# Cross-attention with eight-wide heads on one core: the score matmuls for the softmax maxima as 32-row strips instead of block diagonals

## The reference

```python
Q = _split_heads(q @ Wq.T)          # q = layernorm(x)
K = _split_heads(k @ Wk.T)          # k = v = ctx
V = _split_heads(v @ Wv.T)
scores = einsum('bhqd,bhkd->bhqk', Q, K) / HEAD_DIM ** 0.5
scores = where(attention_mask == 0, NEG_INF, scores)
attn = softmax(scores, axis=-1)
out = einsum('bhqk,bhkd->bhqd', attn, V)     # heads side by side again
x = x + out @ Wo.T
x = x + ffn_top2_of_8(layernorm(x))  # silu(h @ w1.T) * (h @ w3.T) @ w2.T
```

## Time and profile before

| what | value |
|---|---|
| median of 3 runs | 288.39 us (286.16 to 289.48) |
| span of the profiled execution, first to last instruction | 289.2 us |
| quartet 0: front, ticks | to 23.2 us, 23.2 to 40.0 |
| quartet 1: front, ticks | 40.0 to 47.0, 47.0 to 71.0 |
| quartet 2: front, ticks | 71.0 to 78.0, 78.0 to 103.0 |
| quartet 3: front, ticks | 103.0 to 109.0, 109.0 to 147.0 |
| last ticks (`u` = 4) | 147.0 to 182.8 |
| experts and results | 182.8 to 289.2 |

### The profile page before, as it was taken

One profiled execution on the slowest core, in us unless ns is written; L12 is line 12 of the kernel. 1 busy time (PEld: TensorE's weight loads), 2 busy tenths in 40 slices (PEclk: granted clock), 3 DMA queues, 4 the chain that ended last, 5 costly groups with the idle time before them and its releaser, 6 DMA issues.

```text
span 289.2 us, 5289 instructions
## 1 busy us (share of the span) xinstructions
PE 220.1 (76%) x1445; PEld 161.4 (56%) x1445; DVE 214.5 (74%) x619; ACT 131.9 (46%) x291; POOL 109.8 (38%) x120
## 2 busy tenths in 40 slices
PE   0787779998989988887667674688787789997620
PEld 0663456666757665665336542477566668886410
DVE  4779966688759867895977786568895568775596
ACT  5777127554665448342145546243334435453300
POOL 4310350121403070105486556104556565555530
PEclk9996579999999999979756799589899999999855
DMA  6954411353033302331602110421342232211807
GB/s 216 318 233 118 131 35 28 92 125 86 9 98 96 94 0 67 87 100 47 207 9 67 46 39 29 99 47 30 77 79 76 82 84 73 80 52 26 236 5 217
DMA packets 38108, 26.33 MB, mean 91 GB/s; under 512 B 4748, under 2 KB 35726, under 8 KB 37696
## 3 DMA queue, kind: packets, MB, share of 16 engines
q1 hardware_dynamic: 34848, 19.76, 25.5%
q0 software_dynamic: 2656, 5.40, 6.1%
q10 hardware_dynamic: 576, 0.83, 0.9%
HBM read 12.32 MB, written 6.31 MB: 64 GB/s over the span
## 4 chain that ended last, share of the span: by engine, by line
PE 42%; DVE 30%; issue 10%; SPq 8%; DMA 4%; ACT 2%; POOL 1%; another core or an unknown queue 1%; DVEq 0%; ACTq 0%; POOLq 0%
SPq L427 8%; PE bank L528 8%; DVE m_neg L1411 6%; PE bank L759 4%; PE bank L760 3%; PE bank L733 3%; PE bank L652 3%; DMA bd<-st 3%; PE bank L746 3%; PE bank L736 3%; PE bank L693 2%; PE bank L676 2%; PE bank L734 2%; PE bank L679 2%; PE bank L534 2%
## 5 line engine op out<-in xcount | busy, mean ns | idle before, releaser
L1411 DVE TENSOR_REDUCE m_neg<-bank 128x4 f32<-128x512 f32 x64 | 43.5, 684 | 15.4 <-PE bank L693 15.0
L1048 POOL DMA_INDIRECT ys<-big x39 | 38.1, 976 | 40.0 <-DVE big L1447 19.2
L923 ACT ACTIVATE big<-bank 128x512 f32<-128x512 f32 x64 | 37.4, 597 | 20.9 <-PE bank L679 20.0
L797 ACT ACTIVATE st<-bank 128x128 fp32r<-128x128 f32 (+1 forms) x78 | 22.6, 330 | 31.6 <-PE bank L746 16.1
L1004 POOL DMA_INDIRECT xg<-rows,rows_i x24 | 24.6, 1027 | 31.8 <-DVE rows_i L1218 11.6
L693 PE MATMUL bank<-bd,st 128*128 128x512 f32 x64 | 31.1, 509 | 4.7 <-DMA bd<-st 3.8
L676 PE MATMUL bank<-m_bd,ones_b 128*128 128x512 f32 x64 | 31.3, 489 | 2.1 <-ACT big L923 1.9
L759 PE MATMUL bank<-bd,st 128*128 x78 | 24.3, 332 | 9.8 <-DVE big L1447 6.2
L1355 DVE SCALAR_TENSOR_TENSOR st<-st_hi,cst,bank 128x512 fp32r<-128x512 f32 x32 | 23.3, 747 | 11.3 <-ACT st_hi L797 9.0
L1026 POOL TENSOR_TENSOR m_bd<-mT,cst 128x512 fp32r<-128x512 f32 x16 | 17.3, 1110 | 30.1 <-DVE mT L1334 30.0
L679 PE MATMUL bank<-bd,st 128*128 128x512 f32 x64 | 27.1, 423 | 0.0
(11 more groups left out here) (174 smaller groups left out, 514.0 us busy)
## 6 DMA issues: line engine op xcount, KB each, us to landing
bd<-st SPq DMA_DIRECT2D x126, 64.0 KB, 2.0
big<-xg SPq DMA_DIRECT2D x39, 64.5 KB
raw<-in_L_ffn_w SPq DMA_DIRECT2D x2, 1024.0 KB, 9.3
raw<-ys SPq DMA_DIRECT2D x6, 256.0 KB
x_all<-in_x SPq DMA_DIRECT2D x4, 256.0 KB, 4.5
rows<-in_mask_BxS_if POOLq DMA_DIRECT2D x4, 256.0 KB, 5.2
ctx_all<-in_L_ffn_w SPq DMA_DIRECT2D x1, 1024.0 KB
ctx_all<-in_ctx SPq DMA_DIRECT2D x3, 256.0 KB, 5.2
```

The lines of the kernel that those rows point to most:

```text
L923: nc.scalar.activation(prob[n % 2][:, NJ * g:NJ * (g + 1), :].rearrange("p h q -> p (h q)"), s2[k % 2][:, :], ACT.Exp, scale=SCALE).then_i ...
L1048: pool.indirect_dma_start(ys, bass.IndirectOffsetOnAxis(xt[n % XR][:, D:RW].bitcast(I32), 0), y_sb[n % YR], None, bounds_check=PAIRS - 1, ...
L1411: nc.vector.tensor_reduce(m_neg[:, H * (b - 1) + NJ * g:H * (b - 1) + NJ * (g + 1)], s1[k % s1_ring(u)][:, :].rearrange("p (j q) -> p j q" ...
```

## The change

The `s1` product no longer uses a block diagonal. At tick `g` the strip of 32 rows that holds head j = g of all four stacks is used by itself: four matmuls of 32 rows, 128 columns of weights (queries) and 128 moving columns (keys), one for each group i, each into its quarter of the same bank. All four lie on the same strip of the array (`tile_position=(32 g, 0)`); tick by tick the strip moves on. So what a bank holds at tick g is heads (i, g) for i = 0 to 3 instead of heads (g, j), and the reduce writes its four results 4 apart. The block diagonals of the keys go: 62 DMAs of SP, 2 of POOL and their waits, three clears of ACT, and the interleaved order of the remaining DMAs. Two waits for `s1` are dropped, and one for `s2` is added ahead of the fifth piece of expert weights, since `w3_lo` lies in the stacks.

```diff
-        def bd_slot(k, n):
+        def bd_slot(n):
 
-            return bd[:, 3 * (1 - k) + n % 3, :].rearrange("p (g j q) -> p g j q", g=NG, j=NJ)
+            return bd[:, 3 + n % 3, :].rearrange("p (g j q) -> p g j q", g=NG, j=NJ)
...
-            def block_diagonal(k, n):
+            def block_diagonal(n):
 
                 u, b = divmod(n, QB)
-                stacks_in(sp, u, k)
+                stacks_in(sp, u, 0)
                 if n >= 3:
 
-                    sp.wait_ge(s1_full if k else s2_full, NG * (n - 2))
+                    sp.wait_ge(s2_full, NG * (n - 2))
                 else:
-                    sp.wait_ge(bd_cleared, 3 if k else 6)
-                for j in range(2 if k and n == 0 else NJ):
+                    sp.wait_ge(bd_cleared, 3)
+                for j in range(NJ):
...
-                for k, b in ((1, 0), (1, 1), (1, 2), (0, 3), (1, 3)):
-                    if k and u < NQ:
-                        block_diagonal(1, QB * u + b)
-                    if not k and u >= 1:
-                        block_diagonal(0, QB * (u - 1) + b)
+                if u >= 1:
+                    block_diagonal(QB * (u - 1) + 3)
                 if u < NQ:
-                    block_diagonal(0, QB * u)
-                    block_diagonal(0, QB * u + 1)
-                    block_diagonal(0, QB * u + 2)
+                    for b in range(3):
+                        block_diagonal(QB * u + b)
...
-                            if g == 0:
-                                if b == 1:
-                                    stacks_in(pe, u, 0)
-                                    stacks_in(pe, u, 1)
-                                diagonal_in(pe, 1, n)
+                            rows = slice(R * g, R * (g + 1))
+                            if b == 1 and g == 0:
+                                stacks_in(pe, u, 0)
+                                stacks_in(pe, u, 1)
                             if k >= s1_ring(u):
                                 pe.wait_ge(max_done, k - s1_ring(u) + 1)
-                            nc.tensor.matmul(s1[k % s1_ring(u)][:, :], st[:, u % 2, 0, g, (b - 1) * S:b * S],
-                                             bd_slot(1, n)[:, g, :, :].rearrange("p j q -> p (j q)"),
-                                             start=True, stop=True).then_inc(s1_full, 1)
+                            for i in range(NG):
+                                last = nc.tensor.matmul(s1[k % s1_ring(u)][:, i * P:(i + 1) * P], st[rows, u % 2, 0, i, (b - 1) * S:b * S],
+                                                        st[rows, u % 2, 1, i, (b - 1) * S:b * S], start=True, stop=True, tile_position=(R * g, 0))
+                            last.then_inc(s1_full, 1)
...
-            clear_diagonal(0)
-            clear_diagonal(1)
+            act.wait_ge(in_c, 16)
...
-                    act.wait_ge(s1_full, NG * B)
...
-            clear_diagonal(2)
...
-            stacks_in(pool, 0, 1)
-            pool.wait_ge(bd_cleared, 3)
-            for j in range(2, NJ):
-                rows = slice(R * j, R * (j + 1))
-                pool.dma_start(bd_slot(1, 0)[rows, :, j, :].bitcast(F32), st[rows, 0, 1, :, 0:S].bitcast(F32)).then_inc(first_half, 16)
...
+                if k == NB // 4:
+                    dve.wait_ge(s2_full, NG * QB * (NQ - 1))
...
-                            nc.vector.tensor_reduce(m_neg[:, H * (b - 1) + NJ * g:H * (b - 1) + NJ * (g + 1)],
-                                                    s1[k % s1_ring(u)][:, :].rearrange("p (j q) -> p j q", j=NJ), X, ALU.max,
+                            nc.vector.tensor_reduce(m_neg[:, H * (b - 1):H * b].rearrange("p (i j) -> p i j", j=NJ)[:, :, g],
+                                                    s1[k % s1_ring(u)][:, :].rearrange("p (i q) -> p i q", i=NG), X, ALU.max,
                                                     negate=True).then_inc(max_done, 1)
```

More of the change, by code:

```diff
@@ L345, in program @@
         bd_cleared = sem("bd_cleared")
-        kbd_ready = [sem(f"kbd_ready{k}") for k in range(3)]
         qbd_ready = [sem(f"qbd_ready{k}") for k in range(3)]
@@ L349, in program @@
         mhl_ready = sem("mhl_ready")
-        first_half = sem("first_half")
         mbd_ready = sem("mbd_ready")
@@ L377, in stacks_in, with diagonal_in @@
                     taken(engine, ("st", u, k))
[L379 to L383, removed]
+        def diagonal_in(engine, n):
+            engine.wait_ge(qbd_ready[n % 3], 16 * NJ * (n // 3 + 1))
         x_d = x.rearrange("(u b) s d -> u s b d", b=QB)
@@ L414, in _ @@
                 sp.dma_start(raw[k], w).then_inc(in_w13, 16)
-            def block_diagonal(k, n):
+            def block_diagonal(n):
                 u, b = divmod(n, QB)
-                stacks_in(sp, u, k)
+                stacks_in(sp, u, 0)
                 if n >= 3:
-                    sp.wait_ge(s1_full if k else s2_full, NG * (n - 2))
+                    sp.wait_ge(s2_full, NG * (n - 2))
                 else:
-                    sp.wait_ge(bd_cleared, 3 if k else 6)
-                for j in range(2 if k and n == 0 else NJ):
+                    sp.wait_ge(bd_cleared, 3)
+                for j in range(NJ):
                     rows = slice(R * j, R * (j + 1))
-                    sp.dma_start(bd_slot(k, n)[rows, :, j, :].bitcast(F32), st[rows, u % 2, k, :, b * S:(b + 1) * S].bitcast(F32)
-                                 ).then_inc((kbd_ready if k else qbd_ready)[n % 3], 16)
+                    sp.dma_start(bd_slot(n)[rows, :, j, :].bitcast(F32), st[rows, u % 2, 0, :, b * S:(b + 1) * S].bitcast(F32)
+                                 ).then_inc(qbd_ready[n % 3], 16)
             for u in range(NQ + 1):
@@ L668, in _ @@
                             if g == 0:
-                                diagonal_in(pe, 0, n)
+                                diagonal_in(pe, n)
                             if k >= 2:
@@ L679, in _ @@
                             nc.tensor.matmul(s2[k % 2][:, :], st[:, (u - 1) % 2, 1, g, b * S:(b + 1) * S],
-                                             bd_slot(0, n)[:, g, :, :].rearrange("p j q -> p (j q)"),
+                                             bd_slot(n)[:, g, :, :].rearrange("p j q -> p (j q)"),
                                              start=False, stop=True).then_inc(s2_full, 1)
@@ L1346, in _ @@
                         for n in range(QB * (u - 1) - 3, QB * (u - 1)):
-                            diagonal_in(dve, 1, n)
-                            diagonal_in(dve, 0, n)
+                            diagonal_in(dve, n)
                     for k, (is_k, g) in enumerate(stacks(u)):
```

## The result

| | before | changed |
|---|---|---|
| median | 288.94 us (6 runs, 286.16 to 291.12) | 302.48 us (6 runs, 301.54 to 318.81) |
| ratio, 95% interval | | 1.051 (1.044 to 1.057) |
| a repetition: ratio, 95% interval | | 1.046 (1.035 to 1.058) |

The change costs 13.5 us; 300.4 was forecast, with 291 to 313 as the range. The profile shown is of the same kernel run again: span 300.3 us, clock 0.859. Where both are listed, a time lies 1.8 us above the span (302.14 and 300.3), so the profiled execution of before, span 289.2, took about 291 us. It was 2 us above its median, not 0.8 as the prediction has it.

A forecast was written before the change was run, and what follows sets the result against it. PE was taken to bound quartets 1 and 2; stage terms of -0.2, +4.6, +5.2 and +2.4 us summed to +12.0 on 289.2, so 301.2 us profiled and 300.4 for the median, range 291 to 313.

The forecast's parts named there:

- What bounds: PE bounds the ticks of quartets 1 and 2, DVE quartet 0; in quartet 3 they take turns.
- Removal, 1.95 us: Waits for block diagonals that come off: 0.2 us in quartet 0, 1.75 us in quartets 1 to 3.
- The added tick, +0.45 and +0.25: PE time four strips add per tick through weight loads and form changes: +0.45 us, or +0.25 at g = 1.
- the way back: Return from strips to full matmuls in each tick: 0.25 us from the last strip's start.
- Rival 1: Strips change form for free and overlap: +0.20 us a tick, 293.4 us in all; chance 0.19.
- rival 2: No load overlap within a strip: 0.16 us a pair, about +0.60 a tick, 313 us in all; chance 0.14.
- Rival 3: A 32-row weight load costs a quarter, strips stream at 0.055 us: faster, 284.8 us in all; chance 0.07.
- rival 4: Slower 128-column streaming, or half clock in quartets 1 and 2: +0.9 us a tick, 322 us; chance 0.08.
- By stage: Net change of the ticks per quartet: -0.2, +4.6, +5.2 and +2.4 us for quartets 0 to 3, +12.0 in sum.
- Quartet 0's missing gain: PE starts its first `s1` 0.8 us earlier, mostly beside DVE's memset; 0.2 us taken as gain.
- mean of 0.40: Average added PE time over the four ticks g of a batch: +0.40 us a tick.
- The base: The profiled execution, 289.2 us, was taken as 0.8 us above the median of the runs.

The follow-up runs named there:

- x3: The changed kernel with each tick's four strips replaced by one full 128-row matmul of 512 columns on the undivided stacks, no key diagonals: 286.82 us, 0.997 of before.
- x4: The changed kernel with each tick's four strips replaced by four full 128-row matmuls of 128 columns, a weight load each: 290.47 us, 1.005 of before.
- x7: The changed kernel with each tick's four strip matmuls replaced by one of 32 rows and 512 columns: 298.46 us, 1.035 of before.
- x1: The changed kernel run again without edit, for a profile at full clock: 302.51 us, 1.046 of before.
- x10: The kernel before with strips in quartet 0 alone and key diagonals from quartet 1 on: 290.74 us, 1.011 of before.
- x6: The changed kernel with the strips of two ticks issued together at every odd g, alternating between two strips and banks: 306.45 us, 1.064 of before.
- x8: As x6, but the four matmuls of the first strip are issued before the four of the second: 306.59 us, 1.062 of before.

## Why the prediction was right

By its own steps:

- **What bounds**: right. Quartets 1 and 2, where PE was 90% busy and more, took 10.4 of the 13.6 us.
- **Removal, 1.95 us**: right in total (x3: 2.1 us between medians, interval from a gain of 0.7% to a loss of 0.2%). By place it was less good: x3 is 0.5 us shorter than before in quartet 1 (I had 1.0), 0.5 in quartet 2 (0.35) and not shorter in quartet 0 (0.2). In quartet 1 the second wait stood ahead of the ticks of b = 4. Against the first profile, x3 takes 1.0 us less up to their first `s1` (13.4 for 14.4), but 0.5 more from there to their last (3.85 for 3.34). Quartet 3 is 0.9 to 2.2 us shorter, where I had 0.4, but that stage varies by more than 1 us from one profile of the same kernel to the next.
- **The added tick, +0.45 and +0.25**: mechanism right, size too small. Measured +0.56 and +0.35. The term that was mis-sized is the way back. I took 0.25 us from the last strip's start to where the full matmul streams; the records of the single matmuls have the last strip at 52.98, 0.39 after the first, and L670, which follows L667 by 0.23, at 53.51, so L667 streams from 53.28: 0.30. The strips took the other 0.06 (0.39 for 0.33): the record of the first is 0.05 us longer than the others' (0.32 for 0.27), which fits a load with nothing to hide under.
- **Rival 1** (the form is free) and **rival 2** (strips that share rows don't overlap) are out. x4 with loads and no form change is at 290.5, x7 with the form change and one load at 298.5, and strips follow each other at 0.11 us, as full matmuls of 128 columns do. From the second strip of a tick to the fourth it is 0.23 us in x1, where 0.16 a pair would make 0.32. Here, then, the rule of the Trainium skill ("TensorE: Matmul & The Clock Gate", Part 3) that a load overlaps only a matmul on other rows doesn't show as a price. The rule of the Trainium skill ("TensorEngine Tiling (Array Packing)", "Tiling Modes") that changing the mode drains TensorE fits: 0.40 us a tick in x7.
- **Rival 3** (loads cheaper by rows) and **rival 4** (strips at 0.21, or the half clock in quartets 1 and 2) are out by the same 0.11 and by the granted clock of 1.00 there.
- **By stage**: quartet 1 +5.2 (forecast +4.6), 2 +5.2 (+5.2), 3 +1.3 to +2.6 (+2.4), 0 +0.6 (-0.2). The first two were near for two reasons, and one is luck. The ticks of b = 4 cost 0.6 us (4.4 in x1 for 3.85 in x3, first `s1` to last), and I had 0.8. The 12 ticks before them cost 5.0 (18.3 for 13.3, from the first L670 to the first `s1` of b = 4), 0.42 each and not the 0.51 of the two prices above, because there is a third kind of tick that I left out: at g = 0 from b = 2 on, small matmuls follow the strips, and the tick costs only 0.26 to 0.36 more (1.42 for 1.16 and 1.43 for 1.07). So the mean of 0.40 was nearly right, with two terms too small and one kind of tick overlooked. 5.0 and 0.6, with a last tick up to 0.2 longer and less the 0.5 that x3 gains, make the 5.2. Quartet 0's missing gain is DVE's: its memset (23.18 to 24.94 in x1) still stood ahead of the first reduce (25.23), 4.39 us after the last stack matmul in both kernels. Its loss of 0.6 is the one wait shown under x10.
- **The base**: the profiled execution was 2.1 us above the median, not 0.8; from the median of the runs the sum gives 288.9 + 12.0 = 300.9 against 302.5 measured.

## What to carry to other kernels

Price a matmul in another tile form by what stands around it: one strip among full matmuls cost 0.40 us of TensorE time a visit, more than the three extra loads (0.2 us) and nearly twice a full 512-column matmul, and the operand that it saved had been built by DMAs that were nearly hidden. Strips were cheap where many of them, on different rows and into different banks, followed each other with no full matmul between (eight in the time of four in x6, 16 in 0.70 us below); that this pays in time, no run here shows. A queue's share in the chain that ended last was not a saving here: 8% in one profile and 2% in the next of the same kernel, beside a PE over 90% busy, and without half of the issues the time fell by at most 0.7%.

## What I had not expected

- Strips on different rows run side by side, also when they are issued one strip after the other. That PE runs what is queued in order, as the description of the kernel has it, doesn't hold between them: in x8 the eight start in pairs 0.02 us apart or less, though four of one strip are issued before four of the other. At the start of quartet 0 of the changed kernel the 16 matmuls of four ticks, on four strips and into four banks, are done in 0.70 us (weight loads first, then matmuls; start, length):

```profile
23.11 0.59 PEld L684 LDWEIGHTS bank<-st 32*128 32x128 f32 x16 [2.31 <-issue]
23.14 0.70 PE L684 MATMUL bank<-st 32*128 32x128 f32 x16 [1.92 <-DVE st L1339]
```

Four on one strip need 0.39 + 0.27 = 0.66 us, so the four strips overlap nearly wholly. Run one after the other they would need about 16 x 0.11 = 1.8 us. The kernel had no use for it: DVE's memset and then its reduce, at 0.69 us for each tick, came next. In x6 and x8 the same holds for pairs. A tick of the changed kernel can't have it, since its four heads share a strip. Whether four strips on different rows may write the four quarters of one bank at once, no run here shows.

- Half as many changes of form made the kernel slower (x6), by 4 us. Two ticks issued together on PE must wait for two reduces of DVE, and the granted clock of quartet 3 was lower with them.
